# Computing 24 of the 72 routed tiles between the steps of the last three attention blocks

## The reference

```python
x = x + attn(layernorm(x)) @ w_o + b_o
h = layernorm(x).reshape(B * S, D)                      # 4096 tokens
topv, topi = top_k(h @ gate_w + gate_b, 2); gw = softmax(topv)
hid = relu(einsum('td,edf->etf', h, W1) + b1)           # D = 128, F = 512, E = 8
moe = sum over the two chosen e of gw * (hid[e] @ W2[e] + b2[e])
```

## Time and profile before

| | us |
|---|---|
| runs, median of 3 | 706.08 (704.54 to 709.23) |
| the profiled execution | 706.26 |
| its span, first to last instruction | 704.5 |
| loop of `layer_one`, one iteration | about 23 |
| tail: from `turn_back(7)` to the end of `place(7)` | 465.5 to 526.1 |
| first row load of `experts` | 539.1 |
| first and last result of a routed tile | 547.1 and 680.9 |

### The profile page before, as it was taken

One profiled execution on the slowest core, in us unless ns is written; L12 is line 12 of the kernel. 1 busy time (PEld: TensorE's weight loads), 2 busy tenths in 40 slices (PEclk: granted clock), 3 DMA queues, 4 the chain that ended last, 5 costly groups with the idle time before them and its releaser, 6 DMA issues. The chain is left out here.

```text
span 704.5 us, 18257 instructions
## 1 busy us (share of the span) xinstructions
PE 569.9 (81%) x5428; PEld 439.4 (62%) x5429; DVE 401.6 (57%) x1364; ACT 384.8 (55%) x792; POOL 344.8 (49%) x396
## 2 busy tenths in 40 slices
PE   1578998775999945999999999977632999999960
PEld 0234454343999934566766766655522999999960
DVE  6237899974333301345777777783643666565546
ACT  0226787764566512465656656633312888888830
POOL 1246567754000003243476676662454668777750
PEclk9999999965899985999999999985555999999995
DMA  9810001012622133022022122121112222222219
GB/s 283 291 36 1 27 34 45 33 52 77 176 69 67 48 115 151 1 46 48 17 62 63 32 61 63 32 61 39 29 36 76 70 71 74 74 69 71 78 45 343
DMA packets 72071, 54.03 MB, mean 77 GB/s; under 512 B 25816, under 2 KB 63520, under 8 KB 71600
## 3 DMA queue, kind: packets, MB, share of 16 engines
q1 hardware_dynamic: 60400, 34.36, 17.1%
q0 software_dynamic: 6432, 13.25, 5.8%
q10 hardware_dynamic: 5152, 5.34, 2.3%
HBM read 30.30 MB, written 22.62 MB: 75 GB/s over the span
## 5 line engine op out<-in xcount | busy, mean ns | idle before, releaser
L1951 POOL DMA_INDIRECT y_dram<-x_y,x_to x72 | 72.3, 1004 | 37.1 <-DVE x_y L2061 33.9
L1268 POOL DMA_INDIRECT rows_dram<-u_row,u_slots x64 | 63.1, 986 | 55.4 <-DVE u_slots L1823 39.2
L1989 PE MATMUL x_py<-w,x_h 128*128 x576 | 76.2, 275 | 0.1
L2050 DVE TENSOR_SCALAR x_h<-x_pc,x_bT 128x128 f32<-128x128 f32 x144 | 43.9, 345 | 49.2 <-PE x_pc L1977 49.1
L1989 PEld LDWEIGHTS x_py<-w,x_h 128*128 128x128 f32 x576 | 70.0, 192 | 0.3 <-issue 0.3
L1339 PE MATMUL u_py<-u_hh,cwo 128*128 128x512 f32 x128 | 64.0, 595 | 0.0
L2019 ACT ACTIVATE x_held_w<-w 128x512 f32 x72 | 45.3, 630 | 23.9 <-PEq L1187 14.0
L1553 ACT ACTIVATE u_hh<-u_pz 128x512 f32<-128x512 f32 x64 | 36.8, 595 | 36.1 <-PE u_pz L1331 35.9
L2026 ACT ACTIVATE x_h<-x_pa,x_bT 128x128 f32<-128x128 f32 x144 | 45.0, 363 | 12.8 <-PE x_pa L1977 12.6
L1977 PE MATMUL x_pa<-x_xT,x_held_w 128*128 128x128 f32 x288 | 44.8, 279 | 0.0
L1977 PE MATMUL x_pc<-x_xT,x_held_w 128*128 128x128 f32 x288 | 44.6, 278 | 0.0
(11 more groups left out here) (337 smaller groups left out, 1469.0 us busy)
## 6 DMA issues: line engine op xcount, KB each, us to landing
x_xs<-rows_dram SPq DMA_DIRECT2D x72, 65.0 KB
w<-in_mw SPq DMA_DIRECT2D x2, 2048.0 KB, 10.2
cwt<-in_cw SPq DMA_DIRECT2D x1, 2560.0 KB, 10.4
xs_dram<-zero SPq DMA_DIRECT2D x1, 2304.0 KB, 16.2
e_xs<-xs_dram SPq DMA_DIRECT2D x36, 64.0 KB
eo_dram<-e_y SPq DMA_DIRECT2D x36, 64.0 KB, 1.5
x_dram<-x SPq DMA_DIRECT2D x8, 256.0 KB, 2.0
x1t<-x_dram SPq DMA_DIRECT2D x8, 256.0 KB, 4.7
```

The lines of the kernel that those rows point to most:

```text
L1268: pool.indirect_dma_start(rows_dram, bass.IndirectOffsetOnAxis(ap=slots[:, q, k, u:u + 1], axis=0), row[:, q, k, u, :], None).then_inc(sen ...
L1951: pool.indirect_dma_start(y_dram, bass.IndirectOffsetOnAxis(ap=to[t % R][:], axis=0), y[:, t % R, :], None).then_inc(sent[t % R], 16)
L1989: last = nc.tensor.matmul(py[q][:, 0:D], h[:, q, k * P:(k + 1) * P], w2[:, bass.ds(e * FF + k * D, D)], start=(k == 0), stop=(k == KF - 1))
L2050: last = nc.vector.tensor_scalar(h[:, q, k * P:(k + 1) * P], pc[q][:, (k - KH) * P:(k - KH + 1) * P], bT[:, bass.ds(e * KF + k, 1)], 0.0, ...
```

## The change

After four blocks (AB = 4) each expert's region holds a known number of rows. `deal_early`, on DVE in iteration 6 behind `place(3)`, rounds them down to whole tiles and makes a table of the first AT = 24 of them. These tiles are loaded into eight buffers (`load_row`, on SP) and computed inside the tail, by `turn_row`, `first_row` and `second_row` on PE, `gained_row`, `hold_row` and `hidden_row` on ACT, `hidden_row`, `weigh_row` and `result_row` on DVE, and `scatter_row` on POOL. The iterations 8 to 10 of the loop are replaced by an order written out for each engine, in which the steps of the blocks and those of the tiles alternate. Twelve of the tiles have their last DVE step behind `place(7)`. They use the banks of the shared experts (`pz[0]`, `pz[1]`, `py`) and bank e, one each, and the second bias is weighed on DVE instead of POOL. `deal` follows the last tile; it takes off the rows already used, and deals EB = 48 tiles, which `experts` computes as before.

The expert weights are loaded behind the second and the third block's reload of the values, not at the head. The transposed first bias (`bT`) is made at the end of `typed_experts`.

```diff
 XR = 3
 ET += -ET % XR
+AB = 4
+AT = (2 * AB * SB * P - E * (P - 1)) // P
+AT -= AT % XR
+EB = ET - AT
 ROWS = E * T + E * P
 RW = D + 2
...
-sp.dma_start(ew2[:], a["mw"][:, M_W2:, :].rearrange("p m d -> p (m d)")).then_inc(late_loaded, 16)
-sp.dma_start(ew1[:], a["mw"][:, 0:M_W2, :].rearrange("p m d -> p (m d)")).then_inc(late_loaded, 16)
...
+def load_row(t):
+    if t == 0:
+        sp.wait_ge(dealt, 1)
...
+    after(sp, vy_made, t - VU + 1)
+    o = sp.value_load(early_row[0:1, t:t + 1], min_val=0, max_val=ROWS - P)
+    sp.dma_start(vx[t % VU][:], rows_dram[bass.ds(o, P), :]).then_inc(v_loaded[t % VU], 16)
+
+for i in range(NB - 1):
+    store_v(i)
+    load_v(i)
+    if i == 1:
+        sp.dma_start(ew2[:], a["mw"][:, M_W2:, :].rearrange("p m d -> p (m d)")).then_inc(late_loaded, 16)
+    if i == 2:
+        sp.dma_start(ew1[:], a["mw"][:, 0:M_W2, :].rearrange("p m d -> p (m d)")).then_inc(late_loaded, 16)
+for t in range(VU):
+    load_row(t)
+store_v(NB - 1)
+load_v(NB - 1)
+for t in range(VU, AT):
+    load_row(t)
+sp.wait_ge(late_loaded, 32)
 sp.wait_ge(ended, 1)
...
+def scatter_row(t):
+    pool.wait_ge(vy_made, t + 1)
+    pool.wait_ge(vto_made, t + 1)
+    pool.indirect_dma_start(y_dram, bass.IndirectOffsetOnAxis(ap=vto[t % XR][:], axis=0),
+                            vy[:, t % XR, :], None).then_inc(v_sent[t % XR], 16)
...
+carried(NB - 1)
+added(NB - 3)
+scatter_row(0)
+send(NB - 3, 0, 0)
+send(NB - 3, 0, 1)
+scatter_row(1)
+send(NB - 3, 0, 2)
+send(NB - 3, 0, 3)
+send(NB - 3, 1, 0)
+added(NB - 2)
+root2(NB - 2)
+send(NB - 3, 1, 1)
+scatter_row(2)
+send(NB - 3, 1, 2)
+scatter_row(3)
+send(NB - 3, 1, 3)
+scatter_row(4)
+scatter_row(5)
+send(NB - 2, 0, 0)
+send(NB - 2, 0, 1)
+scatter_row(6)
+send(NB - 2, 0, 2)
+added(NB - 1)
+root2(NB - 1)
+send(NB - 2, 0, 3)
+scatter_row(7)
+send(NB - 2, 1, 0)
+scatter_row(8)
+send(NB - 2, 1, 1)
+scatter_row(9)
+send(NB - 2, 1, 2)
+scatter_row(10)
+send(NB - 2, 1, 3)
+scatter_row(11)
+send(NB - 1, 0, 0)
+scatter_row(12)
...
+def turn_row(t):
+    if t == 0:
+        pe.wait_ge(dealt, 1)
+    pe.wait_ge(v_loaded[t % VU], 16 * (t // VU) + 16)
+    claim("e")
+    nc.tensor.transpose(pe_[:, 0:P], vx[t % VU][:, 0:D], ident[:]).then_inc(v_turned, 1)
+    free["e"] = (vxT_made, t + 1)
+
+def first_row(t):
+    pe.wait_ge(vxT_made, t + 1)
+    pe.wait_ge(v_held, t + 1)
+    if t == 0:
+        pe.wait_ge(hh_made, NH * NB)
+    for z, made, summed, ks in ((pz[0], va_made, va_summed, range(KH)), (pz[1], vc_made, vc_summed, range(KH, KF))):
+        after(pe, made, t)
+        for n, k in enumerate(ks):
+            last = nc.tensor.matmul(z[:, n * P:(n + 1) * P], vheld[:, t % VV, k * P:(k + 1) * P], vxT[:, t % 2],
+                                    start=True, stop=True)
+        last.then_inc(summed, 1)
+
+def second_row(t):
+    q = t % 2
+    e = pe.value_load(early_expert[0:1, t:t + 1], min_val=0, max_val=E - 1)
+    if t == 0:
+        pe.wait_ge(late_loaded, 32)
+        pe.wait_ge(yT_made, NB)
+    after(pe, vy_made, t)
+    pe.wait_ge(va_made, t + 1)
+    pe.wait_ge(vc_made, t + 1)
+    for k in range(KF):
+        last = nc.tensor.matmul(py[:, 0:D], vh[:, q, k * P:(k + 1) * P],
+                                ew2[:, bass.ds(e * FF + k * D, D)], start=(k == 0), stop=(k == KF - 1))
+    last.then_inc(vy_summed, 1)
+
 early()
...
+turn_row(0)
+turn_back(NB - 1)
+turn_p(NB - 2, 0)
+turn_p(NB - 2, 1)
+first_row(0)
+scores(NB - 2, 1)
+turn_h(NB - 3)
+turn_row(1)
+second_row(0)
+logits(NB - 3)
+turn_p(NB - 2, 2)
+turn_normed(NB - 1)
+first_row(1)
+query(NB - 1)
+turn_p(NB - 2, 3)
+keys(NB - 1)
+value_rows(NB - 1)
+attend(NB - 2)
+counts(NB - 3)
+turn_row(2)
+second_row(1)
+first_row(2)
+turn_row(3)
+turn_row(4)
+scores(NB - 1, 0)
+turn_o(NB - 2)
+first_row(3)
+project(NB - 2)
+second_row(2)
+turn_p(NB - 1, 0)
+first_row(4)
+turn_p(NB - 1, 1)
+turn_row(5)
+second_row(3)
+scores(NB - 1, 1)
+first_row(5)
+turn_row(6)
+second_row(4)
+turn_row(7)
+turn_p(NB - 1, 2)
+turn_h(NB - 2)
+logits(NB - 2)
+turn_p(NB - 1, 3)
+first_row(6)
+attend(NB - 1)
+second_row(5)
+counts(NB - 2)
+first_row(7)
+turn_row(8)
+second_row(6)
+turn_row(9)
+turn_row(10)
+turn_o(NB - 1)
+first_row(8)
+project(NB - 1)
+second_row(7)
+first_row(9)
+second_row(8)
+turn_row(11)
+turn_row(12)
+first_row(10)
+second_row(9)
+turn_row(13)
+turn_h(NB - 1)
+first_row(11)
+logits(NB - 1)
+second_row(10)
...
+
+def gained_row(t):
+    act.wait_ge(v_turned, t + 1)
+    after(act, vc_summed, t - 1)
+    act.activation(vxT[:, t % 2], pe_[:, 0:P], ACT.Identity, bias=gbc[:, 1:2], scale=gbc[:, 0:1]).then_inc(vxT_made, 1)
+
+def hold_row(t):
+    if t == 0:
+        act.wait_ge(late_loaded, 32)
+        act.wait_ge(dealt, 1)
+    named[t] = act.value_load(early_expert[0:1, t:t + 1], min_val=0, max_val=E - 1)
+    after(act, vc_summed, t - VV + 1)
+    act.activation(vheld[:, t % VV], ew1[:, bass.ds(named[t] * FF, FF)], ACT.Copy).then_inc(v_held, 1)
+
+def hidden_row(t):
+    act.wait_ge(va_summed, t + 1)
...
+exps(NB - 2, 0)
+hold_row(0)
+exps(NB - 2, 1)
+probs(NB - 2, 0)
+gained_row(0)
+hold_row(1)
+probs(NB - 2, 1)
+hold_row(2)
+copies(NB - 3)
+hidden_row(0)
+hold_row(3)
+turned_h(NB - 3)
+gained_row(1)
+exps(NB - 2, 2)
+probs(NB - 2, 2)
+normed(NB - 1)
+exps(NB - 2, 3)
+hidden_row(1)
+hold_row(4)
+query(NB - 1)
+probs(NB - 2, 3)
+keys(NB - 1)
+odds(NB - 3)
+gained_row(2)
+hidden_row(2)
+gained_row(3)
+hold_row(5)
+gained_row(4)
+turned_o(NB - 2)
+hidden_row(3)
+exps(NB - 1, 0)
+hold_row(6)
+exps(NB - 1, 1)
+probs(NB - 1, 0)
+hidden_row(4)
+probs(NB - 1, 1)
+gained_row(5)
+hold_row(7)
+hidden_row(5)
+gained_row(6)
+exps(NB - 1, 2)
+hold_row(8)
+copies(NB - 2)
+probs(NB - 1, 2)
+turned_h(NB - 2)
+exps(NB - 1, 3)
+gained_row(7)
+probs(NB - 1, 3)
+hidden_row(6)
+hold_row(9)
+odds(NB - 2)
+hidden_row(7)
+gained_row(8)
+hold_row(10)
+gained_row(9)
+turned_o(NB - 1)
+hidden_row(8)
+gained_row(10)
+hold_row(11)
+hidden_row(9)
+hold_row(12)
+gained_row(11)
+hidden_row(10)
+gained_row(12)
+hold_row(13)
+copies(NB - 1)
+turned_h(NB - 1)
+hidden_row(11)
+gained_row(13)
+hold_row(14)
+hidden_row(12)
+gained_row(14)
+hold_row(15)
+odds(NB - 1)
...
+def deal_early(i):
+    if i != AB + 2:
+        return
+    done = [0]
+    link(nc.vector.tensor_tensor(acount[:], run[:], base[:], ALU.subtract), early_step, done)
...
+    link(nc.vector.tensor_tensor_scan(aend[:], ones[:, 0:E], alens[:], 0.0, ALU.mult, ALU.add), early_step, done)
+    lines = [1, E - 1, AT]
...
+    link(nc.vector.tensor_reduce(agsum[:], agaps[:].rearrange("p n j -> p j n"), AX, ALU.add), early_step, done)
+    nc.vector.tensor_tensor(early_row[:], agsum[:], c[0:1, C_T:C_T + AT], ALU.add).then_inc(dealt, 1)
...
+    after(dve, vy_made, t - 1)
+    nc.vector.tensor_scalar(vbw[:, t % 2], b2[:, bass.ds(named[t] * D, D)], vx[t % VU][:, D + 1:D + 2], None, ALU.mult)                        .then_inc(vbw_made, 1)
+
+def result_row(t):
+    n = t % XR
+    after(dve, v_sent[n], 16 * (t // XR))
+    nc.vector.tensor_copy(vto[n][:], vx[t % VU][:, D:D + 1]).then_inc(vto_made, 1)
+    dve.wait_ge(vbw_made, t + 1)
+    dve.wait_ge(vy_summed, t + 1)
+    nc.vector.scalar_tensor_tensor(vy[:, n], py[:, 0:D], vx[t % VU][:, D + 1:D + 2], vbw[:, t % 2],
+                                   ALU.mult, ALU.add).then_inc(vy_made, 1)
...
+normalise2(NB - 3)
+statistics1(NB - 1)
+hidden_row(0)
+maxima(NB - 2, 2)
+normalise1(NB - 1)
+maxima(NB - 2, 3)
+gate(NB - 3)
+weigh_row(0)
+choose(NB - 3)
+hidden_row(1)
+result_row(0)
+value_rows(NB - 1)
+weigh_row(1)
+divided(NB - 2, 0)
+place(NB - 3)
+divided(NB - 2, 1)
+hidden_row(2)
+result_row(1)
+weigh_row(2)
+maxima(NB - 1, 0)
+hidden_row(3)
+maxima(NB - 1, 1)
+residual(NB - 2)
+result_row(2)
+statistics2(NB - 2)
+hidden_row(4)
+weigh_row(3)
+result_row(3)
+weigh_row(4)
+maxima(NB - 1, 2)
+normalise2(NB - 2)
+maxima(NB - 1, 3)
+hidden_row(5)
+result_row(4)
+weigh_row(5)
+gate(NB - 2)
+choose(NB - 2)
+hidden_row(6)
+divided(NB - 1, 0)
+result_row(5)
+divided(NB - 1, 1)
+place(NB - 2)
+hidden_row(7)
+weigh_row(6)
+result_row(6)
+weigh_row(7)
+hidden_row(8)
+weigh_row(8)
+residual(NB - 1)
+result_row(7)
+statistics2(NB - 1)
+hidden_row(9)
+result_row(8)
+weigh_row(9)
+normalise2(NB - 1)
+hidden_row(10)
+result_row(9)
+weigh_row(10)
+hidden_row(11)
+weigh_row(11)
+gate(NB - 1)
+choose(NB - 1)
+hidden_row(12)
...
```

More of the change, by code:

```diff
@@ L1093, in layer_one @@
     NH = NSH * KF
+    KH = KF // 2
+    VU, VV = 8, 3
     with ExitStack() as st:
@@ new lines, in _ @@
+                result_row(10)
+                place(NB - 1)
+                result_row(11)
+                hidden_row(13)
+                weigh_row(12)
+                weigh_row(13)
+                result_row(12)
+                hidden_row(14)
+                weigh_row(14)
+                result_row(13)
+                hidden_row(15)
+                weigh_row(15)
+                result_row(14)
+                hidden_row(16)
+                weigh_row(16)
+                result_row(15)
@@ new lines, in _ @@
```

(24 more changed lines are left out.)

322 lines of the change are left out of this document (227 added, 95 removed).

## The result

The changed kernel takes 684.44 us (median of 4 runs, 682.77 to 685.51) against 706.75 us for the kernel before (4 runs): a ratio of 0.968, interval 0.964 to 0.972. The forecast was 687.

What follows compares the result with a forecast made beforehand. PE was taken to bound the loop and `experts`, a chain of hand-overs the tail. Terms -45.2 - 4.0 + 2.7 + 0.3 + 4 + 23.2 = -19.0 us on 704.5 gave 685.5, as median 687; range 675 to 705.

Steps and rivals of the forecast that it cites:

- The tiles: In `experts`: 24 fewer tiles at 1.885 us each, 45.2 us less.
- The gather: Head of `layer_one`: without the weight loads the first gather lands after 2.6 us, not 6.6; -4.0 us.
- `deal_early`: In the loop: about 3.3 us on DVE between `place(3)` and `divided(4)`, of which 2.7 go to PE; +2.7 us.
- The tail: Up to the end of `place(7)`: faster PE clock against inserted tile steps; +4 us, bounds -2 and +17.
- friction of 6 us: In the tail: 6 us added for semaphore delays and some 40 register loads at 0.1 to 0.2 us.
- the walk: Written-out order followed through four queues from `turn_back(7)`, PE at full clock: `place(7)` ends at 524.2, against 526.0 before.
- Behind `place(7)`: From `place(7)` to the first load of `experts`: 36.2 us against 13.0, +23.2 us.
- The bare step: Before `experts`: 9.7 us with only DVE and the fillings at work, hidden by nothing.
- The clock stayed high: Rival denied here: PE's clock stays low in the tail, slower by over 1%, 736 at half clock throughout; chance 0.08.
- no queue passed its insertions on: Rival denied here: queues pass every insertion on, the tail grows by DVE's 17 us; 700, chance 0.27 for 694 to 713.
- near 1.00 between 465 and 560: Sign of the forecast: PE's granted clock near 1.00 between 465 and 560 us; near 0.6 in the tail refutes it.
- the second rival: Queues pass every insertion on, so the tail grows by DVE's 17 us: 700; chance 0.27 for 694 to 713.

Runs made afterwards that it cites:

- heads: The changed kernel with the two 2 MB expert weight loads back at the head of `layer_one`, on chip 2: ratio 1.0085 to the kernel before.
- home: The kernel before, unchanged, run on chip 1 with a profile of its own: 706.42 us.
- same_again: The changed kernel, unedited, run again on chip 1: 682.79 us.
- dealmove: The changed kernel with `deal_early` cut in two and moved ahead of the two `low` steps, on chip 2: ratio 1.009 to the kernel before.
- skip: The changed kernel without early tiles in the tail, all 72 left to `experts`, on chip 5: 742.91 us, ratio 0.999 to the kernel before.
- skipfill: As skip, but with 16 unread products of 128 columns per tile on PE in the tiles' places, chip 5: 751.69 us, ratio 1.016 to before.
- nomove: The changed kernel with only seven row loads and no scatters for the early tiles, all 72 tiles computed in `experts`, on chip 1: 726.95 us.

## Why the prediction was right, point by point

*The tiles.* 24 x 1.885 = 45.2; 45.4 measured (133.8 to 88.4). Right.

*The gather.* -4.0; -4.1, with heads as the proof. That is the landing; that the kernel gets all of it rests on everything behind the gather waiting for it. The Trainium skill (DMA: Bandwidth & Descriptors, section Queues, rings and completion order) has each DMA engine change between queues at every packet. I had read from it that the gather would hardly feel the loads; the trace (6.8 against 2.7 us) doesn't bear that reading out.

*`deal_early`.* +2.7; it took 3.1 us on DVE (3.3; it has 16 operations, eight of them linked, not 18 and ten), the loop grew by 2.8 us (and by 2.8 from home to same_again), and the pause stood where it was forecast, 2.58 us before one `turn_o`. dealmove shows it to be the cause of that pause.

*The tail.* +4 forecast, 0.0 measured (-0.2 on chip 1). The term that was mis-sized is the friction of 6 us added to the walk. The walk said 484.8, 509 and 524.2; the trace says 486.9, 512.1 and 526.2, 2 to 3 us more each time. Of these 1.7 were there at the start: `turn_row(0)` stands ahead of `turn_back(7)` and waits for the first row, whose load is issued at 464.9. I had put the order into the walk and left out that the row isn't there yet. Behind that the trace ends 0.3 us above the walk. The register loads aren't short, though; PE's, for one (min/median/max ns):

```profile
L1589 PEldq TENSOR_LOAD <-u_early_expert x24: 296/302/421, 473.0 to 549.8; - x24
```

I had taken 0.1 to 0.2 us each. So they either lie in waits or are made up for elsewhere, as DVE took 46.2 us, for the 51 forecast; no run parts the two. The clock did its part in kind, 0.92 and 0.97 for 0.60: PE's 584 products for the blocks were busy for 26.1 us in this tail instead of 38.6, 12.5 us less (the forecast had up to 12.6 for the 17 steps on the chain alone). The tail as a whole didn't get shorter, so the tiles' steps took as much back. What the clock alone is worth to the chain, no run shows; skip and skipfill show roughly 4 us for clock and filler together.

*Behind `place(7)`.* +23.2; +22.9. The number is right, and the reason half. 27.1 us to the last result (26.5) were put down to POOL's pace and three buffers; nomove, without a scatter of the tiles, takes 25.2. PE is nearly as slow as POOL there: 2.1 us a tile and not 1.885. The bare step was 8.7 (9.7): the sum of `deal` and the fillings as forecast, less 1. First load to first result took 1.0 us more than before, for which the forecast had no term; but on chip 1 it took 0.6 less (8.3 in same_again, 8.9 in home), so I take it for spread between executions and not for a cost of the change, though the granted clock is low in the bare step (0.55).

*Rivals.* The clock stayed high, and no queue passed its insertions on, where nothing disturbed them. The pattern that the Trainium skill warns of (TensorE: Matmul & The Clock Gate, section HAM oscillation) didn't set in: the clock of the filled tail was 0.92 to 1.00 in the four undisturbed traces with tiles. The sign "near 1.00 between 465 and 560" came true only in part: 0.92 in the tail, 1.00 behind it, 0.55 in the bare step. On chip 2 the second rival's picture came true, a tail longer by 25.7 us, with pauses in it that none of the rivals had; the cause stays open.

*The range*, 675 to 705, held both undisturbed measurements. The 736.75 us of chip 2 lie far outside it, and neither the range nor the rivals had such a chip in them: the baseline itself, on which every term was built, is 25 us longer there. That the forecast came out depended on where it was measured, and that part of it is luck.
